# Attention of the second layer, loop over tiles and heads: the mix of four heads split by context block, the queries' low half and their products placed at other units

## The reference

```python
def _L1_xattn_ref(Q, K, Wq_d, W_qk, Wkv_d, Wv_u):
    H, LKV = 16, 32                      # E = 512, HD = 32
    C_q = Q @ Wq_d
    C_kv = K @ Wkv_d
    CqWqk = (C_q @ W_qk).reshape(b, n, H, LKV)
    scores = jnp.einsum('bnhl,bkl->bhnk', CqWqk, C_kv) / jnp.sqrt(jnp.asarray(LKV, dtype=Q.dtype))
    attn = jax.nn.softmax(scores, axis=-1)
    V_up = (C_kv @ Wv_u).reshape(b, nkv, H, HD)
    out = jnp.einsum('bhnk,bkhd->bnhd', attn, V_up)
    return out.reshape(b, n, H * HD)
...
x = x + _L1_xattn_ref(_layernorm(x, axis=-1), ctx_4096, L1_xattn_Wq_d, L1_xattn_W_qk, L1_xattn_Wkv_d, L1_xattn_Wv_u)
x = x + _L1_ffn_ref(_layernorm(x, axis=-1), ...)
```

## Time and profile before

| | us |
|---|---|
| median of 3 runs | 930.41 |
| lowest and highest run | 925.54, 935.86 |
| the profiled execution | 934.58 |
| its span | 932.9 |
| the loop within the span | about 94.9 to 206 |

### The profile page before, as it was taken

The page is one execution under the profiler, slowest core; times in us unless marked ns, Lnnn a source line. Parts: engine busy times, 40 slices in busy tenths (PEclk is TensorE's granted clock), DMA queues, the critical chain, the costliest instruction groups (busy, mean ns, idle before and its releaser), DMA issues. The chain is left out here.

```text
span 932.9 us, 16524 instructions
## 1 busy us (share of the span) xinstructions
PE 805.0 (86%) x5154; PEld 650.2 (70%) x5158; DVE 731.2 (78%) x1719; ACT 522.7 (56%) x1414; POOL 453.4 (49%) x393
## 2 busy tenths in 40 slices
PE   0986687876788899999999999999999998698478
PEld 0375465653367789889888898898898887563246
DVE  8785876878937788797897887887888888459964
ACT  6573585765435666566657557656756756331220
POOL 4637159802322755646745845746737556323010
PEclk9888998998989999999999999999999999997779
DMA  8333136507020210220210220301202101030001
GB/s 317 115 119 107 39 134 230 164 1 249 1 91 1 91 55 15 91 68 0 90 68 0 90 68 18 118 23 53 82 23 90 45 22 68 24 110 1 0 1 45
DMA packets 39113, 68.22 MB, mean 73 GB/s; under 512 B 5729, under 2 KB 18593, under 8 KB 38946
## 3 DMA queue, kind: packets, MB, share of 16 engines
q1 hardware_dynamic: 39074, 67.73, 21.6%
HBM read 62.38 MB, written 5.34 MB: 73 GB/s over the span
## 5 line engine op out<-in xcount | busy, mean ns | idle before, releaser
L2150 DVE TENSOR_SCALAR_CACHE_REDUCE xn<-ctxT,candidate 128x512 bf16<-128x512 f32 x248 | 174.4, 741 | 0.0
L1917 ACT ACTIVATE layer_attention_probs<-xnT,stats 128x512 f32<-128x512 f32 x128 | 94.2, 736 | 129.3 <-DVE stats L2020 129.3
L2032 DVE TENSOR_TENSOR layer_attention_probsT<-bank,layer_attention_probsT 128x512 fp32r<-128x512 f32 x128 | 88.2, 689 | 47.0 <-ACT layer_attention_probsT L1925 45.4
L1703 PE MATMUL bank<-layer_attention_keysT,layer_attention_queriesT 128*128 128x512 f32 x384 | 122.0, 426 | 3.2 <-DVE layer_attention_queriesT L2013 3.1
L1703 PEld LDWEIGHTS bank<-layer_attention_probsT,layer_attention_values 128*128 128x128 f32 x768 | 100.3, 192 | 15.2 <-issue 5.4
L1703 PE MATMUL bank<-layer_attention_probsT,layer_attention_values 128*128 128x256 f32 x768 | 103.7, 285 | 6.6 <-DVE layer_attention_probsT L2032 6.0
L1703 PE MATMUL bank<-layer_attention_wo,layer_attention_headsT 128*128 128x512 f32 x384 | 102.1, 409 | 3.0 <-issue 3.0
L1925 ACT CAST layer_attention_probsT<-bank 128x512 fp32r<-128x512 f32 x128 | 74.8, 585 | 53.2 <-PE bank L1774 53.2
L1703 PE MATMUL bank<-layer_attention_l_wkv,layer_context_parts 128*128 128x256 f32 x768 | 100.1, 283 | 0.0
L1703 PEld LDWEIGHTS bank<-layer_attention_l_wkv,layer_context_parts 128*128 128x128 f32 x768 | 97.4, 189 | 2.5
L1703 PE MATMUL bank<-layer_attention_l_wq,layer_attention_xnT 128*128 128x512 f32 x384 | 93.2, 392 | 0.0
(11 more groups left out here) (313 smaller groups left out, 1755.0 us busy)
## 6 DMA issues: line engine op xcount, KB each, us to landing
layer_attention_l_raw_qo<-in_wqT SPq DMA_DIRECT2D x9, 1024.0 KB, 5.0
xnT<-inverse_sums SPq DMA_DIRECT2D x16, 512.0 KB, 3.6
layer_attention_l_raw_qo<-in_woT SPq DMA_DIRECT2D x8, 1024.0 KB, 7.0
tw_raw<-in_w_gateT SPq DMA_DIRECT2D x8, 688.0 KB, 5.2
tw_raw<-in_w_upT SPq DMA_DIRECT2D x8, 688.0 KB, 4.1
tw_raw<-in_w_downT SPq DMA_DIRECT2D x6, 768.0 KB, 4.6
layer_attention_l_raw_kv<-in_wkvT SPq DMA_DIRECT2D x9, 512.0 KB, 5.0
ternary<-tw_rounded SPq DMA_DIRECT2D x8, 344.0 KB, 2.5
```

What stands on the lines that cost most here:

```text
L1703: last = pe.matmul(out, stationary[f][a], moving[f][b], start=f == 0 and x == 0, stop=f == count - 1 and x == 2)
L1917: a.activation(probs[:, u % 3, :], masked[:, u % 2, :], ACT.Exp, bias=negmax[:, u:u + 1], scale=-1.0, accum_out=sums[:, u:u + 1]).then_inc ...
L2032: v.tensor_tensor(probsT[:, 1, p % 2, :, columns], T[u % 2][:, :].rearrange("p (c q) -> p c q", c=CPB), probsT[:, 0, p % 2, :, columns], A ...
L2150: own(k.nc.vector.tensor_scalar(k.flags[:, r % 2], row_tile(k.ctxT, r), k.candidate[:, r:r + 1].bitcast(F32), 0.0, ALU.is_ge, ALU.add, acc ...
```

## The change

- The mix of a quad is no longer issued as one piece. At unit u with u % 4 = 1 comes context block 0 (4 products), at u % 4 = 2 block 1 (4 products), and at u % 4 = 3 blocks 2 and 3 (8 products). `quads_done` is raised at the end of the last part. The last quad, after the loop, is still made in one piece.
- Pairs 8 to 15 come at units 8, 12, ... 36 instead of 10, 14, ... 38, on PE and ACT.
- DVE takes each pair's queries_low one unit later than PE and ACT have the pair: at units 1, 3, 5, 7, 9, 13, ... 37.

```diff
--- before.py
+++ after.py
@@ -868,6 +868,7 @@
     FIRST_PAIRS = 4
     COUNT_AT = range(6, 62, 7)
     NORM = range(3)
+    MIXED_AT = {1: (0,), 2: (1,), 3: (2, 3)}
     head, tile, batch = lambda u: u % HEADS, lambda u: u // HEADS, lambda u: u // (HEADS * TPB)
     with ExitStack() as s:
         wv, keysT = lw.wv, lw.keysT
@@ -898,7 +899,7 @@
             if u < 8:
                 return (FIRST_PAIRS + u // 2,) if u % 2 == 0 else ()
             p = HEADS // 2 + (u - 8) // 4
-            return (p,) if u % 4 == 2 and p < PAIRS else ()
+            return (p,) if u % 4 == 0 and p < PAIRS else ()
 
         with nc.Block(no_gpsimd_drain=True) as block:
 
@@ -957,21 +958,23 @@
                                             k.ident[:, :])
                     last.then_inc(S_["probsT_psum"], 1)
 
-                def mix(quad):
-
-                    if quad == 0:
-                        pe.wait_ge(S_["queries_low"], FIRST_PAIRS - 1)
-                    elif quad % QUADS == 0:
-                        pe.wait_ge(S_["mixedT_ready"], quad // QUADS)
-                    pe.wait_ge(S_["probsT_ready"], 4 * quad + 4)
-                    for c in range(CPB):
+                def mix(quad, parts):
+
+                    if 0 in parts:
+                        if quad == 0:
+                            pe.wait_ge(S_["queries_low"], FIRST_PAIRS - 1)
+                        elif quad % QUADS == 0:
+                            pe.wait_ge(S_["mixedT_ready"], quad // QUADS)
+                        pe.wait_ge(S_["probsT_ready"], 4 * quad + 4)
+                    for c in parts:
                         for i in range(4):
                             u = 4 * quad + i
                             h = head(u)
                             last = pe.matmul(O[i * HD:(i + 1) * HD, quad % QUADS * P:(quad % QUADS + 1) * P],
                                              values[:, batch(u) * CPB + c, h * HD:(h + 1) * HD], probsT[:, u % 8, c, :],
                                              start=c == 0, stop=c == CPB - 1)
-                    last.then_inc(S_["quads_done"], 1)
+                    if CPB - 1 in parts:
+                        last.then_inc(S_["quads_done"], 1)
 
                 def turn_mixed(t):
 
@@ -1017,8 +1020,8 @@
                     turn(u)
                     for p in pairs_at(u):
                         queries(p)
-                    if u % 4 == 1 and u >= 4:
-                        mix(u // 4 - 1)
+                    if u % 4 in MIXED_AT and u >= 4:
+                        mix(u // 4 - 1, MIXED_AT[u % 4])
                     if u % HEADS == 4 and u > HEADS:
                         turn_mixed(tile(u) - 1)
                     if u % 2 == 1 and u < 2 * CPB:
@@ -1026,7 +1029,7 @@
                     if u == 10:
                         pe.wait_ge(S_["values_ready"], B * CPB)
                         ternary_totals_tensor(k, X)
-                mix(UNITS // 4 - 1)
+                mix(UNITS // 4 - 1, range(CPB))
                 turn_mixed(TILES - 1)
 
             @block.vector
@@ -1090,7 +1093,7 @@
                 for u in range(UNITS):
                     if u + 3 < UNITS:
                         maximum(u + 3)
-                    for p in pairs_at(u):
+                    for p in pairs_at(u - 1) if u else ():
                         queries_low(p)
                     if u % 4 == 3:
                         copy_turned(u)
```

## The result

| | before | after |
|---|---|---|
| median | 929.96 us (4 runs) | 917.61 us (4 runs, 916.26 to 921.39) |
| the profiled execution, its span | 934.58, 932.9 | 916.26, 914.6 |

The ratio is 0.9861, with a 95% interval of 0.9821 to 0.9902. On the median of 930.41 that is 12.9 us less, where the forecast was 7.4 less. The time lies in the range (917 to 930.5), at its lower end, and outside the forecast's own 921 to 926.5. It is what the rival **more than the sum** gave (about 919, chance 0.28).

The account below looks back on a forecast made before the run. No engine was full: PE, DVE and ACT, busy 71 to 79% of the loop, waited for each other in turn. Terms -7.95 - 0.95 + 1.0 + 0.5 = -7.4 us gave 923.0 on the median's scale; range 917 to 930.5.

Parts of the forecast that it names:

- more than the sum: Rival: PE, standing still less, could keep its clock; up to 4 us beyond the sum, about 919; chance 0.28.
- step (1): queries_low a unit later, products two units sooner: DVE's standing ahead of the subtraction goes, -7.95 us.
- step (2): Mix in three parts, gain: scores behind the mix come sooner, counted at half clock for two mixes, -0.95 us.
- step (3): Mix in three parts, cost: two more switches of 0.37 us a quad, +1.0, and a late tile copy, +0.5.
- the forecast's own signs of being wrong: No gaps at later mix parts, loop clock far from 0.91, or maxima waiting for scores as much as for the subtraction.
- ACT has work then: In the mix's gain: at full clock the shorter first part holds PE less, but this was given no gain.
- late copy: ACT's copy of the finished tile waits for the mix's third part; +0.5 us counted at unit 50.
- 0.8 three times: Sign of being right: a new ACT wait near 0.8 us at the finished tile's copy, three times.
- PE gets no new wait for the queries' bank: Claim on the later queries_low: the bank is reused a pair later at the earliest, so no new wait that costs.
- their 2.0: Units 0 to 6: three of DVE's eight waits at queries_low count almost in full, taken as -2.0 us.
- The waits only move: Rival: only the waits in units 0 to 10 come back, the rest become waits for scores; 929 us, chance 0.20.
- PE becomes the bound: Rival: mix switches of over 0.6 us each use up PE's free time in a quad; about 940, chance 0.07.

Follow-up runs that it names:

- e_after: The changed kernel again, no edit, timed beside other kernels on the same chip: median 920.93 us, ratio 0.9862 to before.
- The filler: Kernel before plus eight unused 128x512 products on PE (three at unit 24, three at 30, two at 32): median 932.2 us, ratio 1.0023.
- e_low_pairs: Kernel before with queries_low a unit later and pairs 8 to 15 two units sooner, mix whole: 921.5 us, ratio 0.9902; timed again 0.9905.

## Why the prediction came out as it did

The measured -12.9 is 5.5 more than the -7.4 of the sum. By edits, 1.0 of it is in step (1) and 4.4 in steps (2) and (3). By the slope, some 3 of it are low clock beyond the 0.95 counted, spread over both; the two ways of cutting the miss overlap and don't add.

**Right in mechanism, in part lucky in size, the waits (step 1).** The two edits together measured 9.1 and 8.8 us against 7.95. The standing ahead of queries_low went, as forecast. But these two kernels also have 9.0 and 6.2 us less low clock, which by the slope is 3.3 and 2.3. So the waits themselves are worth about 6, less than the sum had, and a term that step (1) left out made up for it. In the changed kernel the sign passes of unit 34 follow the maximum of unit 37 at once, and the next maximum comes 3.09 us behind that one, where it took 5.28:

```profile
148.26 0.69 DVE L1046 TENSOR_TENSOR layer_attention_queriesT<-bank,layer_attention_queriesT 64x512 fp32r<-64x512 f32 x1
148.99 0.69 DVE L1051 TENSOR_REDUCE layer_attention_negmax<-bank 128x1 f32<-128x512 f32 x1
149.71 2.44 DVE L2146 TENSOR_SCALAR ctxT<-ctxT,sign 128x512 f32<-128x512 f32 x2
152.08 0.67 DVE L1051 TENSOR_REDUCE layer_attention_negmax<-bank 128x1 f32<-128x512 f32 x1
```

**Mis-sized, the clock.** The loop's clock went from 0.91 to 0.98, one of the forecast's own signs of being wrong. The sum counted the clock only in step (2), at -0.95 for two mixes, and left the rest to a rival with a chance of 0.28 and a size of up to 4. In the profile the miss sits where the low clock went. Units 21 to 37 lost 10.2 us of it, 3.8 by the slope, and another 1.15 in one tiny operation (below), where the forecast missed by 4.7. At units 37 to 41, 3.4 us of low clock or 1.3 stand against a miss of 1.06, and up to unit 21 the same 1.3 against 1.05. Over the runs of e_after it is 4.1, which is that rival's number. All of these are the slope's estimates; a run that sets the clock alone is still lacking. The Trainium skill, TensorE: Matmul & The Clock Gate, Part 1, has activity as what lifts the throttle, and of the kernels in the table those with both edits have 83.5 to 91.3 us of low clock against 97.0. The filler at three units, though, raised the clock in its profile's loop and not over its runs (98.9), so here that sentence alone forecasts no time.

**Wrong by its sign, the split (steps 2 and 3).** Together they had +0.55, and the runs show -2.8 to -3.8 on top of the other edits. The switch itself was priced right: every part has its gaps, here the three parts of one quad. (15 quads are split, where step (3) counts 14; the sum doesn't use that number, only the last rival does.)

```profile
124.65 0.16 PEld L973 LDWEIGHTS bank<-layer_attention_probsT,layer_attention_values 128*32 128x32 f32 x8 [0.17 <-issue]
125.01 0.19 PEld L949 LDWEIGHTS bank<-l_keysT,layer_attention_queriesT 128*128 128x128 f32 x1 [0.20 <-issue]
...
125.88 0.16 PEld L973 LDWEIGHTS bank<-layer_attention_probsT,layer_attention_values 128*32 128x32 f32 x8 [0.17 <-issue]
126.24 0.19 PEld L949 LDWEIGHTS bank<-l_keysT,layer_attention_queriesT 128*128 128x128 f32 x1 [0.20 <-issue]
...
127.11 0.38 PEld L973 LDWEIGHTS bank<-layer_attention_probsT,layer_attention_values 128*32 128x32 f32 x16 [0.17 <-issue]
```

Those gaps have no wait in them, so the 0.37 belongs to the change of tile form and not to what PE stood for, as the rule cited in step (3) has it. What failed is "ACT has work then". I gave the sooner scores a worth only at the low clock. With the waits at queries_low gone, DVE takes the scores as they come, and e_low_pairs still has DVE waiting for them (3.2 us, and 5.5 in its second profile) and PE for ACT (11.0 and 11.1), where the changed kernel has 2.3 and 6.5. Of the split's gain, the low clock (88.0 and 90.8 down to 85.8) is worth 0.8 to 1.9 by the slope.

**Near in number, in part by luck, the quads from unit 41.** Forecast +1.5 for gaps and a late copy, and +1.91 came. The gaps are there at the forecast's price, 0.32 and 0.22, but in two quads and not in four: 0.5 in place of +1.0. The late copy's +0.5 didn't come at all. The other 1.4 are DVE's passes beside POOL, which no step had.

**Wrong, two smaller ones.** ACT's copies of the finished tile wait 0.24, 0.60 and nothing, not 0.8 three times (the 2.2 in the row of waits is the last copy, 2.05 in the earlier trace rows). And the sentence that PE gets no new wait for the queries' bank: it stands 3.7 us for queries_low at units 2, 4 and 8.

```profile
103.97 0.54 PEld L930 LDWEIGHTS bank<-layer_attention_latentT,l_wqk 128*128 128x128 f32 x4 [2.35 <-DVE layer_attention_queriesT L1046]
...
112.50 0.53 PEld L930 LDWEIGHTS bank<-layer_attention_latentT,l_wqk 128*128 128x128 f32 x4 [0.98 <-DVE layer_attention_queriesT L1046]
```

In the first units pairs come every second unit, and a subtraction one unit late leaves only one for the bank; at unit 4 a sum of 1.75 us stood ahead of it on DVE. The first units gained their 2.0 all the same: from the first maximum to the mix of unit 9 are 21.27 us before and 18.99 after. Whether an order that avoids this wait gains more wasn't tried.

**The rivals.** "The waits only move" fell with the waits for scores, 9.2 to 2.3. "PE becomes the bound" had about 940 and fell by the time. Its gaps are 0.37 a switch at full clock, under the 0.6 from which it was to decide, and PE's weight loads still stand 8.9 us for ACT.

## What to carry to other kernels

Look at which engine still works when all its waits are gone: that is the next bound, and it decides which costs show, so an edit that costs by itself (the split) can pay behind another. Where engines wait for each other in turn at a lowered TensorE clock, give the clock a term of its own in the sum, priced by the scatter between runs of the kernel before (mean clock and span of each are enough for it), and keep it apart as an estimate. And before a loop is shortened beside another engine's work of fixed length, see what will fall together with that work.

## What the hardware showed that I had not expected

- Two DVE passes of 128x512 from SBUF to SBUF (tensor_scalar, f32) take 0.87 us by themselves and 1.2 to 2.4 in these two profiles beside POOL's tensor_scalar. A DVE operation on 128x8 shows it best. Rows of before:

```profile
152.37 1.34 POOL L394 TENSOR_SCALAR tw_rounded<-tw_raw 128x1376 bf16<-128x1376 f32 x1
152.42 1.31 DVE L2136 TENSOR_SCALAR rank<-enough 128x8 f32<-128x8 f32 x1
```

  It starts 0.05 behind POOL's and ends with it, at 153.7; in the profile after it takes 0.16. Maxima out of a bank (0.69) and the counting passes (0.67 to 0.69) don't change beside POOL. The Trainium skill, SBUF — State Buffer, Who interferes with whom, has this as an exclusive lock on a port pair that VectorE and GpSimd share: the one that issues second is blocked until the first ends, with tensor_scalar among the operations that take it, and tensor_reduce and the accumulating form not. The trace agrees in all three.
- Executions of one kernel differ by several us outside the changed loop: 729.4 and 735.0 us from the loop's end to the last instruction in two profiles of the changed kernel. A difference of two single profiles says nothing until it is split by place.
